# Set-up work of an attention and expert kernel placed between the first four steps of its first stage

## The reference

```python
xn = layernorm(x)
# attention, 16 heads of 32 features, latent size 128
c      = layernorm(einsum('bhsd,hld->bhsl', xh, Wdkv)) * ln_g + ln_b
q_lat  = einsum('bhsd,hdl->bhsl', xh, einsum('hij,hlj->hil', Wq, Wuk))
w      = softmax(causal(einsum('bhsl,bhtl->bhst', q_lat, c) / sqrt(128)))
v      = einsum('bhsl,hld->bhsd', c, Wuv)
attn   = (einsum('hed', Wo_h) of w @ v, heads joined) @ Wo.T + bo
# experts: the best 2 of 8 per row
ffn    = mean over the chosen 2 of relu(xn @ expert_w[e] + expert_b[e])
out    = x + attn + ffn
```

## Time and profile before

| | us |
|---|---|
| median of 3 runs | 1577.1 (1576.34 to 1578.09) |
| the profiled execution, device time | 1581.08 |
| its span, first to last instruction | 1579.3 |
| TensorE busy | 1505.3 (95%) |
| VectorE busy | 1139.3 (72%) |
| ScalarE busy | 901.5 (57%) |
| GpSimd busy | 582.1 (37%) |

### The profile page before, as it was taken

One profiled execution on the slowest core, in us unless ns is written; L12 is line 12 of the kernel. 1 busy time (PEld: TensorE's weight loads), 2 busy tenths in 40 slices (PEclk: granted clock), 3 DMA queues, 4 the chain that ended last, 5 costly groups with the idle time before them and its releaser, 6 DMA issues.

```text
span 1579.3 us, 42865 instructions
## 1 busy us (share of the span) xinstructions
PE 1505.3 (95%) x12544; PEld 810.1 (51%) x12545; DVE 1139.3 (72%) x2385; ACT 901.5 (57%) x1629; POOL 582.1 (37%) x725
## 2 busy tenths in 40 slices
PE   5799989999999999999999999999999999999998
PEld 2788844545444444444444444444444455554443
DVE  4788778887778777777777777777777344444478
ACT  1677756666666666666666666666666623333200
POOL 2444412232545445432222322232222366666400
PEclk8799979999999999999999999999999999999999
DMA  6589951223322232222322233222322256654499
GB/s 155 163 269 269 261 159 52 70 65 83 87 65 72 61 91 79 71 65 69 95 72 69 63 86 84 72 65 70 93 72 71 73 161 215 199 171 159 150 406 363
DMA packets 156337, 198.06 MB, mean 125 GB/s; under 512 B 45280, under 2 KB 94560, under 8 KB 155904
## 3 DMA queue, kind: packets, MB, share of 16 engines
q1 hardware_dynamic: 114720, 98.23, 21.8%
q10 hardware_dynamic: 27936, 61.38, 12.7%
q0 software_dynamic: 13632, 37.87, 7.5%
HBM read 109.13 MB, written 63.12 MB: 109 GB/s over the span
## 4 chain that ended last, share of the span: by engine, by line
PE 79%; DVE 8%; issue 4%; DMA 3%; POOL 2%; ACT 1%; SPq 1%; another core or an unknown queue 1%; DVEq 0%; ACTq 0%; POOLq 0%
PE PS L1277 29%; PE PS L1405 29%; PE PS L1454 12%; DVE pm L989 5%; PE PS L1478 5%; PE PS L1436 2%; DMA arena<-in_x 1%; POOL arena L623 1%; POOL arena L629 1%; DVE mx L994 1%; SPq L434 1%; DVE mx L993 1%; DVE arena L1008 0%; PE PS L1263 0%
## 5 line engine op out<-in xcount | busy, mean ns | idle before, releaser
L989 DVE TENSOR_REDUCE pm<-PS 128x1 f32<-128x512 f32 (+3 forms) x1280 | 717.1, 602 | 194.9 <-PE PS L1277 180.0
L867 ACT ACTIVATE arena<-PS 128x512 f32<-128x512 f32 (+1 forms) x1152 | 613.4, 574 | 295.1 <-PE PS L1277 273.6
L1277 PE MATMUL PS<-arena 97*64 97x512 f16 (+7 forms) x5120 | 694.4, 353 | 24.6 <-DVE pm L989 21.3
L1405 PE MATMUL PS<-arena 128*33 128x512 f32 (+3 forms) x2560 | 634.9, 530 | 1.0 <-POOL arena L651 1.0
L1277 PEld LDWEIGHTS PS<-arena 97*64 97x64 f16 (+1 forms) x5120 | 330.2, 110 | 412.7 <-DVE pm L989 136.6
L651 POOL TENSOR_SCALAR_AFFINE_SELECT arena<-arena 128x256 f32<-128x256 f32 (+1 forms) x256 | 111.5, 436 | 540.5 <-ACT arena L867 540.4
L1405 PEld LDWEIGHTS PS<-arena 128*33 128x33 f32 x2560 | 160.0, 111 | 80.3 <-POOL arena L651 1.7
L1454 PE MATMUL PS<-w_hi,arena 128*128 x576 | 172.8, 382 | 5.0 <-ACT arena L886 3.5
L886 ACT ACTIVATE arena<-PS 128x1024 f16<-128x1024 f32 x72 | 73.4, 1024 | 151.4 <-remote 111.9
L1277 PE MATMUL PS<-later,deny 128*64 128x128 f16 x1024 | 145.9, 221 | 0.0
L1202 DVE SCALAR_TENSOR_TENSOR arena<-PS,eb_bc 128x512 f32<-128x512 f32 x72 | 49.8, 692 | 122.8 <-PE PS L1454 59.1
(11 more groups left out here) (174 smaller groups left out, 1284.8 us busy)
## 6 DMA issues: line engine op xcount, KB each, us to landing
comb_hl<-arena SPq DMA_DIRECT2D x256, 64.0 KB
w_hi<-expert_rows ACTq DMA_DIRECT2D x32, 512.0 KB, 8.3
arena<-q_pieces ACTq DMA_DIRECT2D x90, 128.0 KB
arena<-k_pieces ACTq DMA_DIRECT2D x90, 128.0 KB
v_rows<-w_lo SPq DMA_DIRECT2D x8, 1056.0 KB, 7.6
arena<-in_x SPq DMA_DIRECT2D x16, 512.0 KB, 5.7
xn_rows<-arena SPq DMA_DIRECT2D x16, 512.0 KB, 6.1
q_pieces<-w_hi SPq DMA_DIRECT2D x32, 256.0 KB, 5.3
```

Of the source, the lines that this page charges most:

```text
L867: a.activation(probs[kk % 4][:, a_ * CH:a_ * CH + w], PS[:, s2_bank(k, x), 0:w], ACT.Exp, scale=SCALE).then_inc(s["exp_done"], 1)
L989: v.reduce_max(pm[:, c, r, p:p + 1], PS[:, S1_BANK[n], 0:w], AX).then_inc(s["s1_done"], 1)
L1277: last = t.matmul(PS[h:h + P // 2, bank, cols], lhsT[:, h:h + P // 2], rhs, start=start, stop=stop)
L1405: last = t.matmul(PS[rows_, 6 + c % 2, CH - wds[a]:CH], v_sb[pu % 2][:, j + a, :], probs[pk % 4][:, a * off:a * off + wds[a]], start=p_ in ...
```

## The change

The program of each engine gets a second function, `beside(p)`, which `run_tiles` calls after each of the four steps ahead of the loop.

- TensorE: the products with ones come behind the block products, with banks 4 and 5 exchanged. The combined weights go to banks 6, 7, 0 and 1. The wait for their low parts stands behind step -3, the four matmuls of the output bias (now bank 4) behind step -2, and the waits for the output bias and the key bias rows behind step -1.
- VectorE: behind the diagonal blocks come the value bias, the split query weights, and the means. The low part of the first combined weight follows step -4; the other three and the output bias's product, sum and scaling follow step -3; the key bias rows follow step -2; the last instruction of the output bias follows step -1.
- ScalarE: a square root of one column stands ahead of its first copy, the load of the expert bias ahead of the high parts. High part 0 is made before the first `spread`, part 1 after it, parts 2 and 3 behind step -4. The combined weights are sent behind step -1.
- `bo_c`, `bdo`, `wo_raw` and `wo_t` lie in the second arena, with a buffer of its own for the product (`bo_part`).

```diff
-        def run_tiles(engine, step):
+        def run_tiles(engine, step, beside=None):
             for p in range(-ROWS_AHEAD, 0):
                 step(0, p, True)
+                if beside:
+                    beside(p)
...
+        COMB_BANK = (6, 7, 0, 1)
...  ScalarE
+            act.wait_ge(s["zeroed"], count(1))
+            a.activation(sd[0][:, 0:1], eps[:], ACT.Sqrt)
...
+            act.dma_start(eb_bc[:], expert_b.partition_broadcast(P)).then_inc(s["eb_in"], 16)
+            def comb_high(k):
                 act.wait_ge(s["comb_ps"], count(k + 1))
...
-            act.wait_ge(s["comb_done"], count(KB))
-            act.dma_start(comb_dram, rest).then_inc(s["comb_out"], 16)
+            def beside(p):
+                if p == -4:
+                    comb_high(2)
+                    comb_high(3)
+                if p == -1:
+                    act.wait_ge(s["comb_done"], count(KB))
+                    act.dma_start(comb_dram, rest).then_inc(s["comb_out"], 16)
+            comb_high(0)
             spread(0, 0)
-            run_tiles(act, step)
+            comb_high(1)
+            run_tiles(act, step, beside)
...  VectorE
+            dve.wait_ge(s["ones_ps"], count(1))
+            v.tensor_copy(bv_bc[:], PS[:, 4, :]).then_inc(s["fold_done"], 1)
             dve.wait_ge(s["wqo_in"], count(16 * 2 * HK))
...          (the split of bdq and bdg, unchanged)
+            means(0, 0, range(CT))
+            def key_bias():          # the former lines 947 to 954, then bk_done
+            def out_bias():          # the former lines 960, 961 and 970
+            def comb_low(k):         # the former line 976 for one k
+            def beside(p):
+                if p == -4:
+                    comb_low(0)
+                if p == -3:
+                    for k in range(1, KB):
+                        comb_low(k)
+                    out_bias()
+                if p == -2:
+                    key_bias()
+                if p == -1:
+                    dve.wait_ge(s["bob_ps"], count(1))
+                    v.scalar_tensor_tensor(out=bo_bc[:], in0=PS[:, 4, :], scalar=1.0 / TOP, in1=bo_bc[:],
+                                           op0=ALU.mult, op1=ALU.add).then_inc(s["bob_done"], 1)
...  TensorE
-            t.matmul(PS[:, 5, :], ones, bwuv, start=True, stop=True)
-            t.matmul(PS[:, 4, :], ones, bwuk, start=True, stop=True)
             pe.wait_ge(s["wc_done"], count(1))
...          (the block products)
+            t.matmul(PS[:, 4, :], ones, bwuv, start=True, stop=True)
+            t.matmul(PS[:, 5, :], ones, bwuk, start=True, stop=True).then_inc(s["ones_ps"], 1)
...
+            def beside(p):
+                if p == -3:
+                    pe.wait_ge(s["comb_done"], count(KB))
+                if p == -2:
+                    pe.wait_ge(s["boc_done"], count(1))
+                    for k in range(KB):
+                        last = t.matmul(PS[:, 4, :], bo_c[:, k:k + 1].to_broadcast([P, P]), wo_t[:, k, :],
+                                        start=k == 0, stop=k == KB - 1)
+                    last.then_inc(s["bob_ps"], 1)
+                if p == -1:
+                    pe.wait_ge(s["bob_done"], count(1))
+                    pe.wait_ge(s["bk_done"], count(1))
```

More of the change, by code:

```diff
@@ L125, in layer_kernel @@
         center = t0(P)
+        t0 = carve(arena2)
+        bo_c = t0(KB)
+        bo_part = t0(KB * P)
         bdo = t0(KB * P).rearrange("p (k c) -> p k c", k=KB)
@@ L210, in layer_kernel @@
         s = {n: sem(n) for n in (
[L211 removed]
+            "eb_in eb_done w_in wqo_in g_in wo_in gate_in bias_in boc_done bob_ps bob_done zeroed consts wc_ps wc_done gw_done fold_ps fold_done ones_ps bk_done "
             "wot_ps wot_done comb_ps comb_hi comb_done gates_done dve0 "
@@ L760, in _ @@
                 a.activation(wo_t[:, k, :], PS[:, 6 + k % 2, :], ACT.Copy).then_inc(s["wot_done"], 1)
-            for k in range(KB):
+            act.dma_start(eb_bc[:], expert_b.partition_broadcast(P)).then_inc(s["eb_in"], 16)
+            def comb_high(k):
                 act.wait_ge(s["comb_ps"], count(k + 1))
-                a.activation(comb_hl[:, 0, k, :], PS[:, 4 + k, :], ACT.Copy, scale=WS).then_inc(s["comb_hi"], 1)
+                a.activation(comb_hl[:, 0, k, :], PS[:, COMB_BANK[k], :], ACT.Copy, scale=WS).then_inc(s["comb_hi"], 1)
             def spread(chunk, u):
@@ new lines, in key_bias @@
+            def key_bias():
+                v.memset(bk_rows, 0.0)
+                link(v.memset(bk_pick, 0.0))
+                for k in range(KB):
+                    r, c = slice(P // KB * k, P // KB * k + 2), slice(P * k, P * (k + 1))
+                    v.memset(bk_pick[r, c], 1.0)
+                    link(v.tensor_copy(bk_rows[r, :], PS[r, 5, c]))
+                    r = slice(P // KB * k, P // KB * k + 1)
+                    last = v.tensor_tensor(bk_rows[r, :], PS[r, 5, c], bk_rows[r, :], ALU.subtract)
+                last.then_inc(s["bk_done"], 1)
@@ L1058, in step @@
                                            op0=ALU.mult, op1=ALU.add).then_inc(s["lg_done"], 1)
-            run_tiles(dve, step)
+            run_tiles(dve, step, beside)
             def routing(n):
@@ L1262, in _ @@
             for k in range(KB):
[L1263 to L1269, removed]
+                t.matmul(PS[:, COMB_BANK[k], :], bdo[:, k, :], wo_t[:, k, :], start=True, stop=True).then_inc(s["comb_ps"], 1)
             pe.wait_ge(s["gates_done"], count(1))
             pe.wait_ge(s["bd_done"], count(1))
+            def beside(p):
[3 more added lines that the diff above has]
+                    pe.wait_ge(s["boc_done"], count(1))
+                    for k in range(KB):
+                        last = t.matmul(PS[:, 4, :], bo_c[:, k:k + 1].to_broadcast([P, P]), wo_t[:, k, :],
[4 more added lines that the diff above has]
+                    pe.wait_ge(s["bk_done"], count(1))
             def halves(bank, cols, lhsT, rhs, start, stop):
@@ L1359, in step @@
                     last.then_inc(s["vv_ps"], 1)
-            run_tiles(pe, step)
+            run_tiles(pe, step, beside)
             def heads(it, more, span):
```

22 lines of the change are left out of this document (6 added, 16 removed).

## The result

The changed kernel takes 1569.76 us (median of 5 runs, 1568.12 to 1572.44), the kernel before on the same chip 1578.09 (5 runs, 1576.34 to 1580.42). The medians differ by 8.3 us. The ratio is 0.9947, 95% interval 0.9935 to 0.9958, so 6.6 to 10.3 us faster. It is a statistic of its own, not the quotient of the medians. The prediction had 8.9. The profiled execution of the changed kernel took 1571.43 us, span 1569.7, 9.6 us under the span before. All numbers here are of fast runs: one run of the kernel before, 1610.29 us at a mean granted clock of 0.937 where the others have 0.984 to 0.989, was in a slower state of the chip and is left out.

A forecast was written before the change was run, and what follows sets the result against it. TensorE was taken to bound 79% of the span's chain, VectorE the set-up. Head start 15.0 less 4.4 given back and 1.7 for the clock made 8.9 us: 1577.1 to 1568.2 us, range 1563.8 to 1572.8.

The forecast's parts named there:

- The head start: Set-up, up to the first normalised tile: five terms bring it 15.0 us sooner, from 43.38 to 28.4.
- terms (2) to (5): Ahead of first tile: key bias rows 3.8, output bias product and sum 1.3, bo scaling to low parts 6.7, sending/table load 1.7 us.
- Term (1): TensorE's set-up: block products no longer behind the products with ones, ending 1.5 us earlier, bounds 0.6 to 2.9.
- Term (5): ScalarE ahead of the first root: sending of the weights and table load leave the path, 1.7 us.
- What is given back: First four steps: VectorE's moved work, the longer path, takes back 4.4 us, leaving 10.6 at the third variance product.
- The clock: TensorE's 4.5 us idle ahead of the loop lowers its clock, costing 1.7 us, bounds nothing to 3.0.
- rival (C): Loop's start: nothing lost to the clock, earlier transfers win a little; gain 11 to 13 us, 1564 to 1566; chance 0.08.
- Rival (E): Loop: clock stays low, 0.5 us lost per us; slower once low more than 21 us behind 47.2; chance 0.03.
- Transfers: Loop's first step: sending the weights (1 MB, 3.8 us of DMA engines) finds room; cost 0, bound 3.8 us.
- (D): Loop's end: transfers hold it, so no head start shows; 1575 to 1577 us; chance 0.07.
- theories N and F: Attention in the repeated combined variant: scatter, 1030 to 1032 us, or earlier start partly given back, 1033 to 1034.

The follow-up runs named there:

- the memsets: Changed kernel with the six memsets of the key bias rows and their picker moved from VectorE to GpSimd; 8.4 us under the kernel before, ratio 0.9950.
- bank 6: Changed kernel with the output bias's matmuls in bank 6, not 4, and TensorE's wait moved to the first tile's values; gain over the kernel before 10.0 us, ratio 0.9938.
- the key bias put ahead: Changed kernel with the key bias rows made ahead of the value bias copy and the tiles again; 7.1 us under the kernel before, ratio 0.9957.
- all-ahead variant: Changed kernel with all work that stood behind the four steps done ahead of the first, same sequence; 3.3 us under the kernel before, ratio 0.9981.
- the filler: Changed kernel with 16 fp16 matmuls, result unread, in TensorE's gap ahead of the loop; 10.7 us under the kernel before, ratio 0.9940.
- no early root: Changed kernel without the square root of one column ahead of ScalarE's first copy; 7.4 us under the kernel before, ratio 0.9955.
- ones ahead: Changed kernel with the two products with ones put back ahead of the block products; 6.7 us under the kernel before, ratio 0.9955.
- the changed kernel's repeat: The changed kernel itself measured again, on chip 4; 8.7 us under the kernel before, ratio 0.9941.
- bank 6 and memsets: Changed kernel with output bias matmuls in bank 6 and the memsets on GpSimd; 10.3 us under the kernel before, ratio 0.9934; again on chip 12, 9.2 us, 0.9949.

## Why the prediction was right

**The head start.** 15.0 predicted, 14.95 measured. First tile 28.4 and 28.43; the last block product ended at 18.2 for 18.0. The terms (2) to (5) are right as a sum: 13.5, and the first tile's distance from the copies fell by 23.80 - 10.23 = 13.57. Term (1) is right for this execution (1.4 us) and too great as a mean: over the twelve executions of kernels with this order the copies start between 18.11 and 19.52, mean 18.9, so 0.7 us against 19.6. That the sum came out to 0.05 us is luck: the clock rose at 16.6, next to the soonest of the twelve. Term (5) has the right size and partly the wrong cause: the variant without the early root has the same first tile. One reading was off without touching the sum: the first tile's matmul at 46.24 is 15.6 us behind the means, which end at 30.6; the 12.8 us are those to its normalisation at 43.38.

**What is given back.** The variance products of the first three tiles were forecast at 33.4, 40.8 and 47.65 and came at 33.60, 40.69 and 47.80; the product of the second tile at 43.8 and 43.71. 10.5 us were left for the forecast 10.6. That VectorE was the longer path is shown by the memsets (1.1 us of its work gone, 1.5 us sooner) and by bank 6: the wait at its end, not the loop's need, holds TensorE. That TensorE is only some 2 us behind is shown by the key bias put ahead: it becomes the path.

Most of the head start only moves VectorE's work to a later place. What the change earns is VectorE's idle time. Three waits of the kernel before are gone: 3.21 and 3.60 us, and the one for the first root behind 41.09:

```profile
43.17 0.18 DVE L1004 RECIPROCAL rs<-sd 128x4 f32<-128x4 f32 x1 [1.86 <-ACT sd L767]
```

They add up to 8.7 us, and from the start of the copies the third product comes 9.1 us sooner. The all-ahead variant, with the same set-up and nothing between the steps, has it 5.7 us ahead of the kernel before: part of the waits go by the order of the set-up alone, and 3.4 us need the work between the steps.

**The clock.** 1.7 predicted, 1.4 measured in the trace (5.80 - 4.43), 1.6 by the filler, and up to 2.2 in the two variants with the same order at this place (no early root, ones ahead). The rival (C), no loss to the clock, is out for this kernel; the variant with fillers, 10.7 us by the medians and 9.4 by the ratio, comes near it. Rival (E) had its mechanism but not its size: the low clock lasted about 3 us of the loop.

**Transfers.** The last product of the stage is 9.45 us ahead of the kernel before, the fourth 9.13: the loop gave nothing back, so (D) is out. The term of 0 is right, its reason is not shown: the DMA share is 0.94 to 1.07 from 46 to 52 us (the windows above), so the sent weights did not find the room that 0.22 promised. What they cost by themselves was not tried.

**The time.** 10.5 - 1.4 = 9.1 us, a little more in the loop, 9.6 in the span; the medians say 8.3 with an interval of 6.6 to 10.3. The forecast for the medians was 8.9.

## Where the better variants' time went

Bank 6 and fillers are 10.0 and 10.7 us under the kernel before where the changed kernel has 8.7 on a chip of that group. They have the lowest ratios but one, but the intervals overlap, so the runs do not tell these variants from the changed kernel. The variants with the memsets on GpSimd gain more in the first stage than in time. The row of VectorE's reduction over a chunk of maxima, one of 128 in attention (the 15th and the last), for the changed kernel's repeat and for the memsets variant:

```profile
310.55 0.17 DVE L1030 TENSOR_REDUCE mx<-pm 128x4 f32<-128x16 f32 x1
...
1230.68 0.17 DVE L1030 TENSOR_REDUCE mx<-pm 128x4 f32<-128x16 f32 x1
```

```profile
308.10 0.17 DVE L1032 TENSOR_REDUCE mx<-pm 128x4 f32<-128x16 f32 x1
...
1230.25 0.17 DVE L1032 TENSOR_REDUCE mx<-pm 128x4 f32<-128x16 f32 x1
```

920.1 us against 922.2, for the same instructions. In the five executions of kernels with these memsets the stretch is 922.1 to 922.3; in the eight executions of the changed kernel and its variants without them and in the kernel before it is 920.0 to 920.8. The difference grows over the whole stage. The five share two things: a GpSimd program six instructions longer ahead of its loops (731 in its count against 725), and a VectorE program six shorter (2379 against 2385). Which of them slows the loops, and how, is open.

Ahead of that mark, from the 3rd of these reductions to the 15th, the executions take 97.7 to 101.0 us, without a pattern that I can name. That scatter is as large as what a variant wins. It and the 2.1 us leave open what theories N and F asked: whether an earlier start is itself partly given back.

## What to carry to other kernels

Count a set-up by the idle time of the engine that carries it: moving work between steps pays where that engine would have waited, and a head start that is paid for later by the same engine is nothing. Look at what the last moved piece holds up: here one bank of PSUM made a result that is first read 1.2 ms later (at 1258 us, by VectorE in the expert stage, not in the final sums) stop TensorE for 4.3 us. With another bank the third product came 1.9 us sooner, and the fourth 3.3, since the clock stayed up as well. Judge a step of 1 to 3 us by landmarks in the trace, and look at the far end too.

## What the runs showed of the hardware

- The same block products, started at 13.7 to 14.0 us in all twelve executions that have them first, end anywhere from 18.1 to 19.5. Their rate doubles at a moment that moves from run to run: 0.43 us per pair of 128-column records before it, 0.22 behind. In five of the twelve executions all twelve pairs ran at the low rate, as here in the one with bank 6 alone:

```profile
13.71 0.77 PE L1284 MATMUL PS<-arena 128*128 128x128 f32 x2 [1.23 <-DVE arena L953]
...
18.53 0.63 PE L1286 MATMUL PS<-arena 128*128 128x128 f32 x2
18.96 1.25 PE L1288 MATMUL PS<-arena 128*128 128x512 f32 x2
```

- The windows gave a granted 1.00 for the set-up's first matmuls in the kernel before, while the rows there show half speed (0.9 us for a 512-column record, as at the granted 0.50 later). In this case the column did not show the clock ahead of its first change.
- The two groups of chips lie 8 us apart, and the expert stage alone accounts for nearly all of that or more: 227.9 us from its first to its last matmul in the first result (changed kernel) and 225.1 on chip 12 (bank 6 and memsets), 217.4 on chip 4 (changed kernel) and 217.5 on chip 7. On chip 4 TensorE is busy throughout (217.47 of 217.50 us), and ScalarE's copies of gathered rows wait only for TensorE; in the kernel before, in its execution of 1581.08 us, they wait 111.9 us in 29 waits of up to 4.8 us for what the trace can't name. Gains of different chips are to be compared only by the kernel before beside them.
